# Scores of the next unit but one placed behind the transposes of a unit's first group

## The chip, the cores and the metric

The kernel runs on one core of one Trainium2 chip. The metric is the device time of one execution in microseconds (us), lower is better. Before the change three runs took 3703.43, 3704.79 and 3709.53 us; their median is 3704.79 us.

## What is computed

A macaron layer over 8 sequences of 1024 tokens of width 256: a feed-forward layer with weight 0.5, an attention layer, and the same feed-forward layer again, each behind a layer norm and with a residual.

```python
x = L0_attn_query                                   # (8, 1024, 256)
x = x + 0.5 * ffn(layernorm(x), w_gate, w_up, w_down)
x = x + attn(layernorm(x), Wq, Wk, Wv, Wo, span_val)
x = x + 0.5 * ffn(layernorm(x), w_gate, w_up, w_down)

def attn(query, Wq, Wk, Wv, Wo, span_val):          # 16 heads of 64
    q, k, v = split(query @ Wq), split(query @ Wk), split(query @ Wv)
    w = softmax(q @ k.T / 64 + causal)
    mask = clip((arange(s) + span_val * s) / 33, 0, 1)
    w = w * mask
    w = w / (sum(w) + 1e-8)
    return merge(w @ v) @ Wo

def ffn(x, w_gate, w_up, w_down):                   # inner width 704
    # every operand is quantised to FP4 in blocks of 16 and back before its product
    return fp4_linear(silu(fp4_linear(x, w_gate)) * fp4_linear(x, w_up), w_down)
```

## The kernel before

The program is written out for each engine by hand, with semaphores. It runs in stages: the weights are prepared, the first feed-forward pass runs, then the attention, then the second feed-forward pass. The change touches the attention alone.

The attention (`attention`) goes over the 8 sequences and, in each, over 8 pairs of attention heads, 64 pairs in all (`over_pairs`; loops in the program, with the first and the last of them written out). A pair is cut into 16 units (`UNITS`): one head and one block of 128 rows of queries, in the order of blocks 7, 0, 5, 1, 6, 3, 4, 2 for each of the two heads. Since the attention is causal, unit (a, j) has 128 (j + 1) columns of scores. A unit's work is this:

- scores (`scores`, L1137, L1138, L1141): TensorE multiplies the queries with the upper and the lower half of the keys (32-bit operands split in two), one chunk of up to 512 columns at a time, 8 of the 16 units having two chunks, and adds the causal mask with one 16-bit matmul of 128 columns. There are two PSUM areas, `s_ps[n % 2]`, so the scores of unit n+2 wait until the exponentials of unit n have been taken from the same area (`exp_done`);
- the row maximum on VectorE (`row_max`, L1319) and the exponentials on ScalarE (`exp`, L1233), which go to `e_rows`;
- transposes of the exponentials in groups of up to four blocks of 128 columns (`turn`, L1151; 24 groups a pair), 32-bit, into `t_ps[i % 3]`; the first of a unit waits for the unit's exponentials, and each for the PSUM buffer that group i-3 leaves (`eT_lo`). ScalarE copies the upper half out as 16-bit (`turn_hi`, L1240), VectorE the rest (`turn_lo`, L1325);
- value products three groups later (`value`, L1167): for each block a matmul of 132 columns with the upper half and one of 66 with the lower half; ScalarE copies the result out (`copy_out`, L1251).

Between them stand side pieces that use one PSUM bank, `side_ps`: transposes of the normalised x (L1097), projections of queries and keys for the next pair (L1066), its values (L1078), transposes of the outputs of the pair before (L1105) and their output product (L1115). Each is copied out in two halves by ScalarE (L1213) and VectorE (L1287) or by VectorE alone, and the next piece waits for that.

The order of all this is written by `pair_steps`, which every engine goes through, taking its own kinds of step. For each unit n it puts `scores` of unit n+2 first, then for each of the unit's one or two groups i: `turn` i, `lo` of group i-1, `max` of unit n+2 (first group only), `value` of group i-3, with `copy` where a unit's last group is done, then the side pieces that `slots` gives to group i; `exp` of unit n+2 comes last. The slots are `WO_SLOTS` in even pairs, `V_SLOTS` in odd ones and `FRESH_SLOTS` in the last pair of a sequence. A step's place in the list is its place in the order of its engine; engines meet at semaphores only.

Of the kernel before, what the change touches and what calls it, by code (L numbers as in the profile page):

```python
# [633 lines left out]
def pair_steps(before, after, fresh, values, rows=False):  # L634

    q, k, v, turn_o, wo, turn_x = ([(kind, c, dg) for c in range(n)] for kind, n, dg in (
        ("q", 2, 1), ("k", 2, 1), ("v", 4, 1), ("o_turn", 2, -1), ("wo", 4, -1), ("x_turn", 4, 1)))
    pieces = (turn_x if fresh else []) + (q + k if after else [None] * 4) + (turn_o if before else [None] * 2)
    if values:
        pieces += v if after else [None] * 4
    else:
        pieces += wo if before else [None] * 4
    slots = {i: [] for i in range(NG)}
    for i, piece in zip(FRESH_SLOTS if fresh else V_SLOTS if values else WO_SLOTS, pieces, strict=True):
        slots[i].append(piece)  # L650
    steps, late_hi, late_lo = [], [], []

    def flush(late):
        steps.extend(late)
        late.clear()

    for n in range(NU):
        more = n + 2 < NU or after
        unit = ((n + 2) % NU, (n + 2) // NU)
        if more:  # L660
            steps.append(("scores",) + unit)
        for i in [i for i, (m, _, _) in enumerate(GROUPS) if m == n]:
            first = GROUPS[i][1] == 0
            flush(late_hi)
            steps.append(("turn", i, 0))
            if i or before:
                steps.append(("lo", (i - 1) % NG, (i - 1) // NG))
            flush(late_lo)
            if first and more:
                steps.append(("max",) + unit)  # L670
            if i >= LAG or before:
                steps.append(("value", (i - LAG) % NG, (i - LAG) // NG))
                m = GROUPS[(i - LAG) % NG][0]
                if LAST_GROUP[m] == (i - LAG) % NG:
                    steps.append(("copy", m, (i - LAG) // NG))
            if before and i in NORM:
                steps.append(("norm", NORM.index(i), -1))
            if rows and i >= ROWS_FROM:
                steps.append(("norm_x", i - ROWS_FROM, 1))
            for piece in slots[i]:  # L680

                flush(late_hi)
                flush(late_lo)
                if piece:
                    steps.append(piece)
                    late_hi.append((piece[0] + "_hi",) + piece[1:])
                    late_lo.append((piece[0] + "_lo",) + piece[1:])
        if more:
            steps.append(("exp",) + unit)
    flush(late_hi)  # L690
    flush(late_lo)
    if not after:
        steps.append(("lo", NG - 1, 0))
        for i in range(NG - LAG, NG):
            steps.append(("value", i, 0))
            if LAST_GROUP[GROUPS[i][0]] == i:
                steps.append(("copy", GROUPS[i][0], 0))
    return steps
# [153 lines left out]
def attention(nc, src, dst, dram, keep):  # L852

    with ExitStack() as ctx:
# [201 lines left out]
        def _(pe):  # L1056
# [123 lines left out]
            def pair(b, r, par, before, after, fresh, twin):  # L1180
                g = b * PAIRS + r

                pe.wait_ge(sem("wo_added"), g * 2 - (2 if par else 4) + AHEAD["wo_added"])
                pe.wait_ge(sem("v_masked"), g * 2 + (2 if par else 4))
                prev = ("k_lo", 2 * g + 2)
                for kind, i, dg in pair_steps(before, after, fresh, par == 1, starts_rows(b, r)):
                    if kind == "scores":
                        scores(i, g + dg, par ^ dg)
                    elif kind == "turn":
                        turn(i, g)  # L1190
                    elif kind == "value":
                        value(i, g + dg, par ^ (dg & 1))
                    elif kind == "x_turn":
                        prev = piece(kind, i, b * QT + QT, b * 4 + 4, 1 - par, 1 - par, prev)
                    elif kind in PIECES:
                        prev = piece(kind, i, g + 1, g - 1, 1 - par, 1 - par, prev)
# [13 lines left out]
        def _(act):  # L1210
# [49 lines left out]
            def pair(b, r, par, before, after, fresh, twin):  # L1260
                g = b * PAIRS + r
                for kind, i, dg in pair_steps(before, after, fresh, par == 1, starts_rows(b, r)):
                    if kind == "exp":
                        exp(i, g + dg, par ^ dg)
                    elif kind == "turn":
                        turn_hi(i, g)
                    elif kind == "copy":
                        copy_out(i, g + dg)
                    elif kind == "x_turn_hi":
                        piece("x_turn", i, b * 4 + 4, None)  # L1270
                    elif kind.endswith("_hi"):
                        piece(kind[:-3], i, g + 1, g - 1, 1 - par)
# [10 lines left out]
        def _(dve):  # L1283
# [82 lines left out]
            def pair(b, r, par, before, after, fresh, twin):  # L1366
                g = b * PAIRS + r
                for kind, i, dg in pair_steps(before, after, fresh, par == 1, starts_rows(b, r)):
                    if kind == "norm_x":
                        norm_x(b + 2, i)  # L1370
                    elif kind == "max":
                        row_max(i, g + dg)
                    elif kind == "lo":
                        turn_lo(i, g + dg)
                    elif kind == "norm":
                        normalise(i, g - 1, 1 - par)
                    elif kind == "x_turn_lo":
                        piece("x_turn", i, b * 4 + 4, None)
                    elif kind.endswith("_lo"):
                        if kind == "wo_lo" and i == 0:  # L1380

                            dve.wait_ge(sem("acc_loaded"), b * 16 + (0 if isinstance(r, int) and r == 0 else 16))
                        piece(kind[:-3], i, g + 1, g - 1, 1 - par)
# [67 lines left out]
```

## Time and profile before

| | |
|---|---|
| median of three runs | 3704.79 us |
| the profiled execution | 3706.25 us, its span 3704.5 us |
| mean granted TensorE clock | 0.984 |
| TensorE matmuls | 3460.5 us (93%), 29924 instructions |
| TensorE weight loads | 3147.8 us (85%) |
| VectorE | 2913.8 us (79%) |
| ScalarE | 2278.6 us (62%) |
| GpSimd | 827.0 us (22%) |

The profile names the engines PE (TensorE matmuls), PEld (TensorE weight loads, which run beside matmuls), DVE (VectorE), ACT (ScalarE), POOL (GpSimd) and SP (SyncE, which issues the DMAs). The busy times are sums over the whole span. A matmul's duration reaches from its start to the end that the profile models for it, so that neighbouring matmuls overlap; how much time one takes in the stream is read from its start to the start of the next one. In a timeline a line that ends in x4 stands for four instructions of one kind.

### The profile page before, as it was taken

The numbers are of one execution on the slowest core, as the hardware profiler recorded it, in microseconds if no ns is written. First come the engines' busy times: TensorE is split into PE (matmuls) and PEld (weight loads), VectorE is DVE, ScalarE is ACT, GpSimd is POOL, SyncE is SP. The second block draws the span as 40 slices with busy tenths as digits, with TensorE's granted clock in tenths as the row PEclk, the third lists the DMA queues.
The fourth block names the chain that finished last, engine by engine and source line by source line (L and its number), as shares of the span: only waits on it lengthen the run. The fifth ranks groups of instructions, "written<-read, shape, count | busy, mean of one in ns | idle before, by whom it ended". The sixth has DMA issues, their size and how long they took to land. (4 is left out here: it accounts for less than half of the span.)

```text
span 3704.5 us, 87366 instructions
## 1 busy us (share of the span) xinstructions
PE 3460.5 (93%) x29924; PEld 3147.8 (85%) x29924; DVE 2913.8 (79%) x4756; ACT 2278.6 (62%) x4086; POOL 827.0 (22%) x834
## 2 busy tenths in 40 slices
PE   0799995999999999999999999999999999599998
PEld 0799995888888888888888888888888888499998
DVE  7899983777877787777777778777777777599996
ACT  1445542777777677767767767776777767254554
POOL 2233221121212212122212212212122112123322
PEclk9999998999999999999999999999999999799999
DMA  6211113454544454454545545545534543211111
GB/s 204 76 57 51 51 43 108 104 119 102 145 112 102 119 128 113 107 140 103 119 104 137 119 103 126 119 102 133 125 91 111 134 103 86 97 47 54 51 51 35
DMA packets 157957, 373.40 MB, mean 101 GB/s; under 512 B 19216, under 2 KB 61072, under 8 KB 157200
## 3 DMA queue, kind: packets, MB, share of 16 engines
q1 hardware_dynamic: 157712, 370.30, 39.1%
q8 instruction: 134, 2.20, 0.3%
q14 instruction: 111, 0.91, 0.1%
HBM read 129.31 MB, written 39.58 MB: 46 GB/s over the span
## 5 line engine op out<-in xcount | busy, mean ns | idle before, releaser
L1240 ACT ACTIVATE at_eT_hi<-at_t_ps 128x512 f16<-128x512 f32 (+3 forms) x1536 | 742.4, 490 | 508.9 <-PE at_t_ps L1151 490.8
L1325 DVE SCALAR_TENSOR_TENSOR at_eT_lo<-at_t_ps,at_eT_hi 128x512 f16<-128x512 f32 (+3 forms) x1536 | 824.7, 548 | 127.6 <-ACT at_eT_hi L1240 112.5
L1233 ACT ACTIVATE at_e_rows<-at_s_ps,at_neg_max 128x1024 f32<-128x1024 f32 (+7 forms) x1024 | 761.5, 744 | 95.5 <-DVE at_neg_max L1319 75.2
L1319 DVE TENSOR_REDUCE at_neg_max<-at_s_ps 128x1 f32<-128x1024 f32 (+7 forms) x1024 | 766.9, 749 | 50.1 <-PE at_s_ps L1141 49.8
L1151 PE MATMUL at_t_ps<-at_ident,at_e_rows 128*128 128x128 f32 x4608 | 773.9, 277 | 0.9 <-DVE at_eT_lo L1325 0.9
L1137 PE MATMUL at_s_ps<-at_kh_st,at_q_st 128*128 128x512 f32 (+2 forms) x1536 | 582.3, 379 | 33.9 <-issue 22.9
L1167 PE MATMUL at_o_ps<-at_v_cols,at_eT_hi 128*128 128x132 f16 x4608 | 610.5, 221 | 0.9 <-ACT at_o_raw L1251 0.9
L1167 PE MATMUL at_o_ps<-at_v_cols,at_eT_lo 128*128 128x66 f16 x4608 | 567.9, 193 | 0.0
L1138 PE MATMUL at_s_ps<-at_kl_st,at_q_st 128*128 128x512 f32 (+2 forms) x1536 | 514.1, 342 | 0.0
L1151 PEld LDWEIGHTS at_t_ps<-at_ident,at_e_rows 128*128 128x128 f32 x4608 | 498.9, 141 | 10.5 <-issue 1.4
L1167 PEld LDWEIGHTS at_o_ps<-at_v_cols,at_eT_hi 128*128 128x128 f16 x4608 | 436.0, 98 | 1.8 <-DVE at_eT_lo L1325 0.7
L1167 PEld LDWEIGHTS at_o_ps<-at_v_cols,at_eT_lo 128*128 128x128 f16 x4608 | 420.9, 98 | 17.6
L1066 PE MATMUL at_side_ps<-at_xT_hi,at_w_qk 128*128 128x512 f32 x1012 | 385.3, 421 | 14.5 <-DVE at_q_lo L1287 6.7
L1137 PEld LDWEIGHTS at_s_ps<-at_kh_st,at_q_st 128*128 128x128 f32 x1536 | 290.0, 189 | 69.2 <-issue 26.6
L1030 POOL TENSOR_TENSOR at_o_sum<-at_o_raw 128x1056 f32<-128x1056 f32 x64 | 133.1, 2079 | 835.1 <-ACT at_o_raw L1251 835.1
L1138 PEld LDWEIGHTS at_s_ps<-at_kl_st,at_q_st 128*128 128x128 f32 x1536 | 291.7, 190 | 24.4
L425 POOL TENSOR_TENSOR ffn_h_q<-ffn_code,ffn_scale 128x704 f32<-128x704 f32 x128 | 175.4, 1391 | 585.8 <-DVE ffn_code L366 585.8
L530 PE MATMUL ffn_gu_ps<-ffn_w_gu_hi,ffn_xT_hi 128*128 128x352 f32 x1024 | 262.3, 337 | 14.5 <-DVE ffn_raw L329 10.0
L467 ACT ACTIVATE ffn_silu<-ffn_gu_ps 128x704 f32<-128x704 f32 x128 | 97.1, 759 | 282.1 <-PE ffn_gu_ps L530 282.1
L530 PE MATMUL ffn_gu_ps<-ffn_w_gu_lo,ffn_xT_hi 128*128 128x352 f32 x1024 | 250.3, 326 | 0.0
L530 PE MATMUL ffn_gu_ps<-ffn_w_gu_hi,ffn_xT_lo 128*128 128x352 f32 x1024 | 249.8, 325 | 0.0
L1066 PEld LDWEIGHTS at_side_ps<-at_xT_hi,at_w_qk 128*128 128x128 f32 x1012 | 193.2, 191 | 59.7 <-DVE at_q_lo L1287 21.3
(185 smaller groups left out, 7045.7 us busy)
## 6 DMA issues: line engine op xcount, KB each, us to landing
at_kh_st<-at_k_hi SPq DMA_DIRECT2D x256, 256.0 KB, 4.5
at_kl_st<-at_k_lo SPq DMA_DIRECT2D x256, 256.0 KB, 5.8
at_w_qk<-w_qk_split SPq DMA_DIRECT2D x65, 512.0 KB, 6.2
at_q_st<-at_q_hi SPq DMA_DIRECT2D x128, 256.0 KB, 3.9
at_q_st<-at_q_lo SPq DMA_DIRECT2D x128, 256.0 KB, 4.9
at_w_v<-w_v_split SPq DMA_DIRECT2D x66, 256.0 KB, 5.7
at_w_out<-w_out_split SPq DMA_DIRECT2D x32, 512.0 KB, 3.7
ffn_x_rows<-in_L_attn_query_dram SPq DMA_DIRECT2D x32, 256.0 KB, 2.8
```

The lines of the kernel that those rows point to most:

```text
L425: nc.gpsimd.tensor_tensor(blocks_of(h_q[:, par, j, :INNER]), blocks_of(code[:, j * INNER:(j + 1) * INNER]), per_block(scale[:, par, j * HB ...
L530: last = nc.tensor.matmul(gu_ps[:, c, 0:HALF_I], xT[a][:, par, kt, j * P:(j + 1) * P], gu[b][:, kt, c * HALF_I:(c + 1) * HALF_I], start=n ...
L1030: nc.gpsimd.tensor_tensor(o_sum[:], o_raw[:, :, :VHI], o_raw[:, :, VHI:], ALU.add).then_inc(sem("o_sum"), 1)
L1066: last = nc.tensor.matmul(bank[:], wts[:, w, s, kt, :], xT[t][:, kt, c * CHUNK:(c + 1) * CHUNK], start=i == 0, stop=i == len(passes) - 1)
L1137: nc.tensor.matmul(out, qs, kh_st[par][a][:, k0:k0 + w], start=True, stop=False)
L1138: last = nc.tensor.matmul(out, qs, kl_st[par][a][:, k0:k0 + w], start=False, stop=not lastc)
L1151: last = nc.tensor.transpose(t_ps[i % TBUF][:, b * P:(b + 1) * P], e_rows[:, n % 4, (k0 + b) * P:(k0 + b + 1) * P], ident[:])
L1167: last = nc.tensor.matmul(o[:, :VPART[s]], eT[s][:, i % EBUF, b * P:(b + 1) * P], v_cols[par][:, k0 + b, a, :VPART[s]], start=k0 + b == 0 ...
L1233: nc.scalar.activation(e_rows[:, n % 4, :w], s_ps[n % 2][:, col:col + w], ACT.Exp, bias=neg_max[:, n % 4:n % 4 + 1]).then_inc(sem("exp_don ...
L1240: nc.scalar.activation(eT[0][:, i % EBUF, :count * P], t_ps[i % TBUF][:, :count * P], ACT.Copy, scale=PSCALE).then_inc(sem("eT_hi"), 1)
L1319: nc.vector.tensor_reduce(neg_max[:, n % 4:n % 4 + 1], s_ps[n % 2][:, col:col + P * (j + 1)], AX.X, ALU.max, negate=True).then_inc(sem("ma ...
L1325: nc.vector.scalar_tensor_tensor(out=eT[1][:, i % EBUF, :count * P], in0=t_ps[i % TBUF][:, :count * P], scalar=PSCALE, in1=eT[0][:, i % EB ...
```

## The change

In `pair_steps` the step `scores` of unit n+2 moves from the head of unit n to a place behind the transposes of the unit's first group: behind `turn`, behind `lo` of the group before, behind the late halves of side pieces, and right ahead of `max` of unit n+2. The condition under which it is issued is the same. `scores` is a step of TensorE alone, so the orders of the other engines stay as they are; on TensorE the first `turn` of a unit and the `scores` change places, and `value` follows the `scores` where it followed the `turn`.

```diff
     for n in range(NU):
         more = n + 2 < NU or after
         unit = ((n + 2) % NU, (n + 2) // NU)
-        if more:
-            steps.append(("scores",) + unit)
         for i in [i for i, (m, _, _) in enumerate(GROUPS) if m == n]:
             first = GROUPS[i][1] == 0
             flush(late_hi)
...
                 steps.append(("lo", (i - 1) % NG, (i - 1) // NG))
             flush(late_lo)
             if first and more:
+                steps.append(("scores",) + unit)
                 steps.append(("max",) + unit)
             if i >= LAG or before:
                 steps.append(("value", (i - LAG) % NG, (i - LAG) // NG))
```

## Rows read from the trace of the kernel before

**Rows 1.** Busy time by window: us, then each engine's busy us (instructions), clock, DMA.

```profile
644.00:3154.00 2510.00, 2459.01 (x22978) 2171.32 (x22977) 1941.95 (x3512) 1774.92 (x3473) 503.56 (x536) 1.00 0.48 115
```

**Rows 2.** Groups by line, TensorE, 1000 to 1500 us: count, busy us, mean ns, idle.

```profile
L1137 PE MATMUL at_s_ps<-at_kh_st,at_q_st 128*128 128x512 f32 (+2 forms) x308 | 116.2, 377 | 3.2 <-issue 2.3 <-DVE at_acc L1313 0.6
...
L1138 PE MATMUL at_s_ps<-at_kl_st,at_q_st 128*128 128x512 f32 (+2 forms) x308 | 102.8, 341 | 0.0
```

**Rows 3.** Timeline of TensorE's matmuls, around unit 6: start us, duration us, instruction.

```profile
1012.90 0.19 PE L1167 MATMUL at_o_ps<-at_v_cols,at_eT_lo 128*128 128x66 f16 x1
1012.93 0.22 PE L1167 MATMUL at_o_ps<-at_v_cols,at_eT_hi 128*128 128x132 f16 x1
1013.00 0.19 PE L1167 MATMUL at_o_ps<-at_v_cols,at_eT_lo 128*128 128x66 f16 x1
1013.02 0.48 PE L1137 MATMUL at_s_ps<-at_kh_st,at_q_st 128*128 128x512 f32 x1
1013.35 0.39 PE L1138 MATMUL at_s_ps<-at_kl_st,at_q_st 128*128 128x512 f32 x1
1013.57 0.40 PE L1137 MATMUL at_s_ps<-at_kh_st,at_q_st 128*128 128x512 f32 x1
...
1014.04 0.23 PE L1141 MATMUL at_s_ps<-at_causal,at_ident_b 128*128 128x128 bf16 x1
1014.11 0.61 PE L1151 MATMUL at_t_ps<-at_ident,at_e_rows 128*128 128x128 f32 x4
1014.55 0.22 PE L1167 MATMUL at_o_ps<-at_v_cols,at_eT_hi 128*128 128x132 f16 x1
```

**Rows 4.** Timeline of TensorE's weight loads at the same place.

```profile
1013.00 0.19 PEld L1137 LDWEIGHTS at_s_ps<-at_kh_st,at_q_st 128*128 128x128 f32 x1
1013.11 0.19 PEld L1138 LDWEIGHTS at_s_ps<-at_kl_st,at_q_st 128*128 128x128 f32 x1
```

**Rows 5.** Timeline of TensorE's matmuls, scores behind a projection.

```profile
1510.42 0.39 PE L1066 MATMUL at_side_ps<-at_xT_hi,at_w_qk 128*128 128x512 f32 x1
1510.65 0.40 PE L1137 MATMUL at_s_ps<-at_kh_st,at_q_st 128*128 128x512 f32 x1
1510.89 0.40 PE L1138 MATMUL at_s_ps<-at_kl_st,at_q_st 128*128 128x512 f32 x1
```

**Rows 6.** Timeline of TensorE's matmuls, scores behind the last transpose of x.

```profile
1234.44 0.27 PE L1097 MATMUL at_side_ps<-at_ident,at_xn 128*128 128x128 f32 x1
1234.47 0.48 PE L1137 MATMUL at_s_ps<-at_kh_st,at_q_st 128*128 128x512 f32 x1
1234.78 0.40 PE L1138 MATMUL at_s_ps<-at_kl_st,at_q_st 128*128 128x512 f32 x1
```

**Rows 7.** Timeline of TensorE's matmuls, transposes of a second group behind value products.

```profile
1005.48 0.19 PE L1167 MATMUL at_o_ps<-at_v_cols,at_eT_lo 128*128 128x66 f16 x1
1005.50 0.41 PE L1151 MATMUL at_t_ps<-at_ident,at_e_rows 128*128 128x128 f32 x2
1005.75 0.22 PE L1167 MATMUL at_o_ps<-at_v_cols,at_eT_hi 128*128 128x132 f16 x1
```

**Rows 8.** Waits of TensorE's weight loads, 1000 to 1500 us: us, times, longest us.

```profile
PEld at_side_ps L1066 <- DVE at_q_lo L1287: 3.3, 12, 0.3
```

**Rows 9.** Waits of VectorE, 1000 to 1500 us.

```profile
DVE at_eT_lo L1325 <- ACT at_eT_hi L1240: 21.2, 70, 0.7
...
DVE at_neg_max L1319 <- PE at_s_ps L1141: 6.7, 27, 0.3
```

**Rows 10.** Timelines of VectorE, ScalarE and TensorE: from unit 6 to unit 8.

```profile
1014.48 1.21 DVE L1319 TENSOR_REDUCE at_neg_max<-at_s_ps 128x1 f32<-128x1024 f32 x1
...
1016.22 1.12 ACT L1233 ACTIVATE at_e_rows<-at_s_ps,at_neg_max 128x1024 f32<-128x1024 f32 x1
...
1017.40 0.50 PE L1137 MATMUL at_s_ps<-at_kh_st,at_q_st 128*128 128x512 f32 x1
```

## The prediction

> **What bounds the kernel now.** I read the page's head first, then the busy time by windows, to see which engine fills the stretch that the edit touches. The attention stretch, from the first scores at 644 us to 3154 us, is two thirds of the span of 3704.5 us; in it TensorE is busy 2459 of 2510 us, VectorE 1942 and ScalarE 1775 us, at a granted clock of 1.00 [rows 1]. So VectorE and ScalarE have room (77% and 71%), and TensorE sets the pace. But a matmul that waits for its weights counts as busy here, so 98% does not say that nothing can be gained: the reader has to go from busy time to the distance between the starts of neighbouring matmuls. That is what the timelines of TensorE are for [rows 3 to 7]. Last I read who waits for whom on TensorE's weight loads and on VectorE [rows 8, 9], and one place where a unit's head does wait [rows 10].
>
> **What the change does to the order.** Per unit it exchanges two blocks on TensorE. (The head of a unit is here the place where its work begins; a pair is a pair of attention heads, 16 units, and takes some 40 us.) Before: (work X of the unit before), scores of unit n+2, transposes of group one, value products. After: X, transposes, scores, value products. Nothing is added or removed: 1024 units, each with the same matmuls, the same semaphores and the same waits. ScalarE and VectorE keep their orders. Both blocks wait at the head for the same exponentials (those of unit n: the scores to overwrite their PSUM banks, the transposes to read their rows), so the head wait stays where it is. Three things can move: the price of the boundaries between blocks, the time at which the scores are there (later by the transposes, up to 0.44 us), and the time at which the transposes are there (earlier by the scores, up to about 1 us). SyncE, GpSimd and the DMA queues are not passed by anything.
>
> **Boundaries, priced from start to start.** Everything below is at the clock of 1.00.
>
> Scores behind value products: the last value matmul starts at 1013.00, the first score matmul at 1013.02, the second at 1013.35: 0.35 us for the two. In a stream the short value matmul takes 0.03 (1012.90 to 1012.93) and a score matmul of 512 columns 0.22 (1013.35 to 1013.57) to 0.23. So 0.09 to 0.10 us is open. The weight loads tell why: the first load starts at 1013.00 and the second at 1013.11, so a 32-bit load takes about 0.11, and a matmul of 0.03 cannot hide it [rows 3, 4]. I take 0.09.
>
> Scores behind a projection of 512 columns: 0.23 and 0.24 us from start to start, nothing open [rows 5].
>
> Scores behind transposes, the new boundary: the trace has it at the few places where transposes of x stand ahead of a unit. 1234.44 to 1234.47 to 1234.78 is 0.34 for the two; in a stream it is 0.11 (four transposes in 0.44, 1014.11 to 1014.55) plus 0.23. Nothing is open: a transpose lasts as long as the load behind it [rows 3, 6].
>
> Transposes behind the causal matmul, which disappears: that matmul holds 0.07 (1014.04 to 1014.11), where a stream of about as many columns (the 132 of a value matmul) takes 0.05 to 0.06 [rows 3]: 0.015 open.
>
> Transposes behind value products, new at the head: two take 0.25 us (1005.50 to 1005.75) where two in a stream take 0.22: 0.03 open [rows 7]. Behind a projection I take nothing, as for the scores, since its 0.23 is longer still [rows 5].
>
> Value products behind the causal matmul, new, and not in this trace. From below: the 16-bit load of a value matmul is hidden behind 0.03 us of another value matmul [rows 3], so nothing is open and the causal matmul takes its 0.05. From above: the first value matmul starts 0.11 after the last of four transposes (1014.11 to 1014.55 is four times 0.11) [rows 3], which would put 0.06 on every unit; but 0.11 is the length of the transpose itself, so it is no sign of a slow load. I take 0.005 open, near the low end, and keep 0.06 for a rival. A gain below nothing is excluded, since the columns have to stream.
>
> **The sum.** How many heads stand behind value products is counted in the code: a unit's head does so unless a slot puts a side piece on the last group before it. With the slots of even pairs that is 9 of 16 units, of odd pairs 8, of the last pair of a sequence 6; the very first and the very last pair have fewer side pieces and 13 such heads each: 31 x 9 + 24 x 8 + 7 x 6 + 26 = 539. A second way to the same term: on the two lines of the score matmuls, which have the same shapes and counts, the mean is 377 ns on the one that comes first and 341 ns on the other; 36 ns x 308 is 11.1 us in 500 us, or 54 ns for each of its 205 units (8 of 16 units have two such matmuls, the others one: 308 / 1.5), 55 us over 1024 [rows 2]. 539 x 0.09 is 49 us, and the 63 heads behind the transposes of the outputs, which have the same long first matmul (0.50) [rows 10], bring the rest. The two agree.
>
> Heads behind value products: before 0.09 + 0.015, after 0.03 + 0 + 0.005, so 0.07 us each, times 539: 37.7 us. The 485 others: before 0 + 0.015, after 0 + 0.005, so 0.01 each: 5 us. Together some 42 us less on TensorE.
>
> Not all of it is kept. Where TensorE waits for a side piece's second half, it arrives earlier and waits longer: 12 such waits, of 0.27 us on average, in 500 us [rows 8], about 60 in the stretch, take back 0.07 each, 4 us. Heads that wait for an exponential [rows 10] may give back 1 us more. That leaves 37 us.
>
> The profiled execution took 3706.25 us (its span 3704.5): 3706 - 37 = 3669. The median of the runs before, 3704.79, lies 1.5 us below the profiled execution, so the forecast for the median is 3668 us, 1.0% faster.
>
> **Where a rule of the skill stands against this.** The trace shows second score matmuls that start 0.33 us behind the first where 0.23 would do, with the load of their weights begun only as the matmul before starts [rows 3, 4]. The Trainium skill, page "TensorE: Matmul & The Clock Gate", section "Step-by-step: what each phase is for", says that TensorE's queue pulls weight loads ahead of matmuls in flight, so that the next tile's weights load while this one's matmul runs. Read as a full cover, it would make every order of blocks cost the same, and the time would stay at 3705; the rows show a cover of one matmul's length only.
>
> **Rivals.**
>
> The order costs nothing, since what I read as open load time is bound to the score matmuls and goes with them wherever they stand. Then nothing moves: 3705 us. For it: every score block that isn't behind a projection has a long first matmul, also the one behind the transposes of x (0.48) [rows 6]. Against it: the start of that one is early by what its length is long by, and the distance over both is the stream's. Chance 0.06.
>
> The gain is made on TensorE and half lost at waits. For it: GpSimd apart, all engines are chained within 2 units, VectorE alone waited 70 times in 500 us for ScalarE's halves of the transposed rows [rows 9]. Against it: most of these waits end long ahead of TensorE's need. It would give 18 us: 3687 to 3697. Chance 0.12.
>
> The open load moves to the value products. Behind the causal matmul each unit would pay 0.06 instead of 0.005: 1024 x 0.055 = 56 us more, 3668 + 56 = 3724. Decided by whether a 16-bit load hides behind a matmul of 128 columns. Chance 0.04.
>
> The other side: late scores hold the next but one head. The scores end up to 0.44 us later, VectorE's maximum follows them, then the exponentials on ScalarE, and the head of unit n+2 waits for these. VectorE waited for scores 27 times in 500 us, about twice in each pair [rows 9]. At unit 8 the exponentials end at 1017.34 and the head starts at 1017.40 [rows 10]. If two heads in each of the 64 pairs, this one and another, paid the whole 0.44: 128 x 0.44 = 56 us, and 3668 + 56 = 3724. It decides where the slack from scores to maximum to exponentials is under 0.44. Against it: at that very place the scores start for the last time at 1014.04, the maximum only at 1014.48 since VectorE is still at other work, it ends at 1015.69, and the exponentials start at 1016.22: about 0.2 us of slack before it and 0.53 behind it, which are 0.7 together [rows 3, 10]. Chance 0.08, with the milder forms, 3700 to 3730.
>
> **How the numbers follow.** Forecast 0.70, within 3655 to 3690 (0.05 to 0.09 us a head behind value products, nothing to 5 us taken back). Half lost 0.12; nothing moves 0.06; slower for one of two reasons 0.12. The range, 3653 to 3700, takes in the first two. About 0.2% (7 us) is what a measurement of this kernel can tell from no change. Faster by more than that, under 3697: 0.70 + 0.10 = 0.80. Within it: 0.10. Slower: 0.10.
>
> **What would show it.** In the profile after: at heads behind value products the first transpose follows the last value matmul by 0.03 and the first score matmul the last transpose by 0.03, with the second score matmul 0.34 behind that transpose, not more; the first value matmul 0.05 to 0.07 behind the causal one. The span of the attention stretch is shorter by about 37 us and the feed-forward passes are unchanged. The mean of the first score line does not fall: these matmuls stay long and only start earlier. ScalarE waits less for transposes of first groups. Wrong would be: 0.11 between causal and value matmul, waits of heads for the exponentials that are longer than 0.1 us at most pairs, or a maximum that follows the scores directly in all units.

## The result and the profile after

The changed kernel took 3710.91 us in the median of 20 runs (3703.27 to 3716.12), the kernel before 3704.52 us in 20 runs (3700.63 to 3709.53). The ratio is 1.0015, 95% interval 1.0009 to 1.0022: no gain, at most a loss of 0.2%. Forecast were 3668 us and a range of 3653 to 3700. The profiled execution of the changed kernel took 3703.27 us (span 3701.5), the shortest of its runs; a second one, of the same kernel, had a span of 3707.0. So single spans of the two kernels, 3704.5 before, can't be told apart, and I read the traces by their steady part instead.

GpSimd sums the outputs once in each pair (L1030, after the change L1028), so the distance of these sums is the length of a pair. The timeline of GpSimd around 1100 to 1200 us, the kernel before:

```profile
1118.57 2.08 POOL L1030 TENSOR_TENSOR at_o_sum<-at_o_raw 128x1056 f32<-128x1056 f32 x1 [3.88 <-ACT at_o_raw L1251]
...
1157.16 2.08 POOL L1030 TENSOR_TENSOR at_o_sum<-at_o_raw 128x1056 f32<-128x1056 f32 x1 [24.14 <-ACT at_o_raw L1251]
...
1195.47 2.09 POOL L1030 TENSOR_TENSOR at_o_sum<-at_o_raw 128x1056 f32<-128x1056 f32 x1 [3.86 <-ACT at_o_raw L1251]
```

and the changed one:

```profile
1119.18 2.08 POOL L1028 TENSOR_TENSOR at_o_sum<-at_o_raw 128x1056 f32<-128x1056 f32 x1 [3.94 <-ACT at_o_raw L1249]
...
1157.78 2.08 POOL L1028 TENSOR_TENSOR at_o_sum<-at_o_raw 128x1056 f32<-128x1056 f32 x1 [24.12 <-ACT at_o_raw L1249]
...
1196.11 2.08 POOL L1028 TENSOR_TENSOR at_o_sum<-at_o_raw 128x1056 f32<-128x1056 f32 x1 [3.94 <-ACT at_o_raw L1249]
```

Before, the two pairs take 38.59 and 38.31 us, 76.90 together; after, 38.60 and 38.33, 76.93. This length of two pairs is the measure below. It stays the same to 0.03 us, although TensorE's blocks are cheaper. The timeline of TensorE at unit 6 of the changed kernel, the answer to [rows 3]:

```profile
1013.51 0.19 PE L1165 MATMUL at_o_ps<-at_v_cols,at_eT_lo 128*128 128x66 f16 x1
1013.54 0.63 PE L1149 MATMUL at_t_ps<-at_ident,at_e_rows 128*128 128x128 f32 x4
1013.93 0.48 PE L1135 MATMUL at_s_ps<-at_kh_st,at_q_st 128*128 128x512 f32 x1
1014.25 0.40 PE L1136 MATMUL at_s_ps<-at_kl_st,at_q_st 128*128 128x512 f32 x1
...
1014.94 0.23 PE L1139 MATMUL at_s_ps<-at_causal,at_ident_b 128*128 128x128 bf16 x1
1015.01 0.22 PE L1165 MATMUL at_o_ps<-at_v_cols,at_eT_hi 128*128 128x132 f16 x1
```

From the last value matmul to the next one it is 1.50 us, where the same two blocks took 1.55 before (1013.00 to 1014.55) [rows 3]: 0.05 us saved. The weight load of the first score matmul now starts with the last transpose, a little before the matmul itself:

```profile
1013.90 0.19 PEld L1135 LDWEIGHTS at_s_ps<-at_kh_st,at_q_st 128*128 128x128 f32 x1
```

so 1013.90 to 1014.25 is 0.35 for a transpose (0.11) and a score matmul (0.23), with 0.01 open instead of 0.09.

Where did it go? The waits of TensorE's weight loads over 644 to 3154 us (us in total, times, longest), before (the row left out on top, a wait of the causal matmul's load that the profile puts down to nothing, is 110.8 us and 111.5 after):

```profile
...
PEld at_side_ps L1066 <- DVE at_q_lo L1287: 21.3, 55, 3.4
PEld at_s_ps L1137 <- issue: 16.6, 9, 3.0
PEld at_s_ps L1137 <- ACT at_e_rows L1233: 14.2, 37, 1.5
...
PEld at_side_ps L1105 <- DVE at_oT_lo L1287: 2.3, 9, 0.3
```

and after:

```profile
...
PEld at_side_ps L1103 <- DVE at_oT_lo L1285: 27.3, 63, 0.5
PEld at_t_ps L1149 <- issue: 25.3, 36, 2.6
PEld at_side_ps L1064 <- DVE at_q_lo L1285: 23.6, 56, 3.0
...
PEld at_t_ps L1149 <- DVE at_eT_lo L1323: 9.3, 19, 1.3
PEld at_t_ps L1149 <- ACT at_e_rows L1231: 5.5, 9, 0.8
```

The wait for the lower half of the output transposes grew from 2.3 to 27.3 us, from 9 times to 63, once in each pair but the first. The waits at the heads of units grew from 16.6 + 14.2 = 30.8 to 25.3 + 9.3 + 5.5 = 40.1, the query's from 21.3 to 23.6. Together that is 37 us more of waiting.

The place of the large one is unit 7: its second side piece, output transposes, must wait until VectorE has taken the lower half of the first one, issued in unit 6. VectorE's timeline there, after the change:

```profile
1015.21 1.23 DVE L1317 TENSOR_REDUCE at_neg_max<-at_s_ps 128x1 f32<-128x1024 f32 x1
1016.35 0.68 DVE L1323 SCALAR_TENSOR_TENSOR at_eT_lo<-at_t_ps,at_eT_hi 128x512 f16<-128x512 f32 x1
1016.95 0.68 DVE L1285 SCALAR_TENSOR_TENSOR at_oT_lo<-at_side_ps,at_oT_hi 128x512 fp32r<-128x512 f32 x1
```

and TensorE's:

```profile
1017.19 0.19 PE L1165 MATMUL at_o_ps<-at_v_cols,at_eT_lo 128*128 128x66 f16 x1
1017.69 0.33 PE L1103 MATMUL at_side_ps<-at_ident,at_o_norm 128*128 128x128 f32 x1 [0.30 <-DVE at_oT_lo L1285]
```

The maximum of unit 8's 1024 columns starts 0.27 us after the causal matmul that ends the scores (1014.94), which is when these are there; the half of group 9 and the half of the output transposes stand behind it, and the last one ends at 1017.63. TensorE starts its last value matmul at 1017.19 and the output transposes only at 1017.69. In the kernel before, the same maximum started 0.44 after the causal matmul [rows 3, 10], because VectorE was busy: 0.2 us of cover, as the prediction counted, against the 0.39 of the four transposes (1013.54 to 1013.93) that the scores now stand behind.

### The profile page after: what moved, and what is told of

Its sections match the earlier page's. It is cut to its first block and busy times, and to the rows that moved or that the text cites. A ratio compares the mean times of both kernels' runs of the same rounds, so it can differ in the third digit from the quotient of the medians.

```text
span 3701.5 us, 87366 instructions
## 1 busy us (share of the span) xinstructions
PE 3431.3 (93%) x29924; PEld 3114.3 (84%) x29924; DVE 2924.5 (79%) x4756; ACT 2261.4 (61%) x4086; POOL 827.3 (22%) x834
## 5 line engine op out<-in xcount | busy, mean ns | idle before, releaser
L1135 PE MATMUL at_s_ps<-at_kh_st,at_q_st 128*128 128x512 f32 (+2 forms) x1536 | 615.4, 401 | 9.7 <-issue 9.7
L1149 PEld LDWEIGHTS at_t_ps<-at_ident,at_e_rows 128*128 128x128 f32 x4608 | 521.1, 141 | 77.1 <-issue 25.3
L1028 POOL TENSOR_TENSOR at_o_sum<-at_o_raw 128x1056 f32<-128x1056 f32 x64 | 133.2, 2082 | 834.7 <-ACT at_o_raw L1249 834.7
L530 PE MATMUL ffn_gu_ps<-ffn_w_gu_hi,ffn_xT_hi 128*128 128x352 f32 x1024 | 262.0, 337 | 15.0 <-DVE ffn_raw L329 10.2
L1064 PEld LDWEIGHTS at_side_ps<-at_xT_hi,at_w_qk 128*128 128x128 f32 x1012 | 192.6, 190 | 62.6 <-DVE at_q_lo L1285 23.6
```

The source lines that it names most:

```text
L530: last = nc.tensor.matmul(gu_ps[:, c, 0:HALF_I], xT[a][:, par, kt, j * P:(j + 1) * P], gu[b][:, kt, c * HALF_I:(c + 1) * HALF_I], start=n ...
L1064: last = nc.tensor.matmul(bank[:], wts[:, w, s, kt, :], xT[t][:, kt, c * CHUNK:(c + 1) * CHUNK], start=i == 0, stop=i == len(passes) - 1)
L1135: nc.tensor.matmul(out, qs, kh_st[par][a][:, k0:k0 + w], start=True, stop=False)
L1149: last = nc.tensor.transpose(t_ps[i % TBUF][:, b * P:(b + 1) * P], e_rows[:, n % 4, (k0 + b) * P:(k0 + b + 1) * P], ident[:])
```

## The experiments

Each was timed 4 to 12 times beside the kernel before (the changed kernel first 20 times); a ratio is to that kernel, whose median lay between 3704.5 and 3707.2 us from one series of measurements to the next, so kernels are compared by ratios or within one series. "Two pairs" is the distance over two of the sums above. In all but the first, the shifted-slot and the short-maximum kernels, a set of units keeps its scores at the head:

```diff
+        if more and n in EARLY:
+            steps.append(("scores",) + unit)
         for i in [i for i, (m, _, _) in enumerate(GROUPS) if m == n]:
...
             if first and more:
-                steps.append(("scores",) + unit)
+                if n not in EARLY:
+                    steps.append(("scores",) + unit)
                 steps.append(("max",) + unit)
```

| kernel | median us | ratio (95%) | two pairs us |
|---|---|---|---|
| before | 3704.52 | | 76.90 |
| changed | 3710.91 | 1.0015 (1.0009 to 1.0022) | 76.93 |
| changed, again | 3707.84 | 1.0002 (0.9992 to 1.0012) | 76.92 |
| unit 6 early | 3695.21 | 0.9964 (0.9951 to 0.9977) | 76.62 |
| unit 14 early | 3711.37 | 1.0013 (1.0004 to 1.0022) | 76.92 |
| units 6, 14 early | 3701.40 | 0.9984 (0.9975 to 0.9993) | 76.66 |
| late: unit 6 alone | 3716.06 | 1.0029 (1.0019 to 1.0039) | 77.23 |
| changed, slots moved | 3743.49 | 1.0098 (1.0082 to 1.0113) | 78.24 |
| before, slots moved | 3749.32 | 1.0116 (1.0101 to 1.0132) | 78.45 |
| changed, four slots moved | 3790.19 | 1.0224 (1.0210 to 1.0238) | 79.79 |
| changed, short maximum | 3687.60 | 0.9946 (0.9932 to 0.9959) | 76.53 |
| before, short maximum | 3696.62 | 0.9974 (0.9963 to 0.9984) | 76.88 |
| late: 0, 1, 4, 7, 10, 12 to 15 | 3694.89 | 0.9967 (0.9955 to 0.9979) | 76.63 |
| late: 2, 3, 5, 8, 9, 11 | 3708.24 | 1.0006 (0.9997 to 1.0015) | 76.95 |
| late: 1, 7, 15 | 3706.11 | 1.0001 (0.9992 to 1.0010) | 76.93 |
| late: 0, 4, 10, 12 | 3699.48 | 0.9983 (0.9974 to 0.9993) | 76.68 |
| late: 4, 10, 12 | 3693.27 | 0.9965 (0.9953 to 0.9977) | 76.61 |
| late: 4, 10, 12, 13, 14 | 3692.81 | 0.9967 (0.9956 to 0.9979) | 76.47 |

**The same kernel again, and units 6 and 14 put back.** `EARLY = (6,)`, `(14,)` and `(6, 14)`.

> The changed kernel once more, as the common ground of the other three runs, and to see whether its first profiled execution (3703 us, the shortest of its runs) is like the rest. Both theories expect 1.001 to 1.002 of the kernel before. Theory A (late halves: the maximum, now later on VectorE, pushes the late halves of side pieces behind it, and TensorE waits at the next side piece) expects the same waits of TensorE for VectorE's output halves as in the first profile, 63 times and some 18 to 27 us, whatever the run. Theory B (clock: the gain is there, but the granted clock falls more often) expects a granted clock under that of the kernel before by 0.005 or more, in a profile that is some 7 us longer than the first.

> The changed kernel with the scores of unit 6 alone back at the head (64 of 1024 units). Theory A: the maximum of unit 8's scores (1.2 us) no longer delays the late half of the first output transposes, so TensorE's wait for it falls from some 27 us to under 8 and the kernel is 12 to 16 us faster than the changed one (18 back, 4 given up for 64 boundaries at 0.07). Theory B and theory C (heads wait for exponentials): no less wait, and 4 us slower than the changed kernel.

> The changed kernel with the scores of unit 14 alone back at the head. Theory A, if the wait at the start of a pair (34 us in the changed kernel against 26 before, at unit 0) is of the same kind: 4 to 8 us back, 4 given up, so within 5 us of the changed kernel. Theory C (the exponentials of unit 0, which follow these scores, hold the head of unit 0): the same size, and ScalarE's waits for the maximum get shorter there. It tells how much of the rest hangs on unit 14; theory B expects 4 us slower.

> The changed kernel with the scores of units 6 and 14 at the head, the other 14 late. Theory A: the sum of the two, 14 to 20 us faster than the changed kernel, which is 0.996 to 0.998 of the kernel before. Theory B: 8 us slower than the changed kernel.

The changed kernel came out at 1.0002, with the same wait in its second trace (27.3 us, 63 times); that speaks against theory B, and its granted clock of 0.984 is that of the kernel before. One unit of sixteen back at the head gives 12.6 us against the changed kernel of the same series, in the expected 12 to 16, and the wait falls:

```profile
PEld at_side_ps L1107 <- DVE at_oT_lo L1289: 12.1, 63, 0.4
```

It did not fall under 8: a part of it hangs on something else. Unit 14 back at the head was 3.5 us slower than the changed kernel, within the 5 us that were given, with two pairs as long as before (76.92). Both together were expected 14 to 20 us faster than the changed kernel and were 6, two pairs taking 0.04 us more than with unit 6 alone, which is 1 us over the kernel; the other 5 us are no longer than what the granted clock does to single executions (see the sum below).

**Unit 6 alone late.** All other units in `EARLY`.

> The kernel before with the scores of unit 6 alone late, in 64 of 1024 units. Theory A: 24 us of waits at the side piece of unit 7 appear, less 4 us for 64 cheaper boundaries: 14 to 20 us slower, ratio 1.004 to 1.006. Rival D gives the same sign, but with the wait at the head of unit 8. If the loss needs all units late, this kernel is within 5 us of the one before.

1.0029, 11 us, with two pairs 0.33 us longer, which is 10.6 us over 32 such lengths; expected were 14 to 20. The sign and the place are right (in its trace the wait for the output's half is 23.9 us, 63 times), so a single late unit in sixteen does harm, and all of it at another unit's side piece.

**The second output transposes one group later.**

```diff
-WO_SLOTS = (0, 2, 4, 7, 9, 11, 13, 16, 19, 21)
-V_SLOTS = (0, 2, 4, 7, 9, 11, 13, 16, 20, 22)
+WO_SLOTS = (0, 2, 4, 7, 9, 12, 14, 16, 19, 21)
+V_SLOTS = (0, 2, 4, 7, 9, 12, 14, 16, 20, 22)
```

and, in the last of the three, slots 2 and 4 as 3 and 5.

> The changed kernel with the second output transposes of a pair one group later (slot 11 to 12) and the first value or output product behind them at slot 14 instead of 13. All scores stay late. Theory A (late halves): TensorE no longer meets the unfinished half at unit 7, which cost 24 us a kernel more than before, so 18 to 28 us faster than the changed kernel, 0.993 to 0.996 of the kernel before. Rival D (the scores of unit 6 are late for a reason of their own, such as the exponentials of unit 8, and the side piece is only where TensorE happens to stand): the wait moves to the head of unit 8 or to slot 14 and nothing is gained.

> The control: the kernel before with the same two slots moved. Its wait at that place was 7 us, so theory A expects 4 to 8 us at most, 0.998 to 0.999; a gain like that of the changed kernel would say that the slots were bad by themselves and that the late scores had no part.

> Like the changed kernel with the two slots moved, and the second query projection at slot 3 instead of 2 and the first key projection at 5 instead of 4. TensorE waits there for the query's lower half 56 times in the kernel before too (22 us). Theory A, taken as a rule for side pieces in general (a piece must not come before VectorE is through with the half of the one before): 15 to 25 us more than with the first move, about 0.988 to 0.990 of the kernel before. Against it: the keys arrive later for the copies that the next pair needs, but those are far from their use.

All three missed, by 1% and more, and on the other side. Of late scores they say little: with the slots moved the changed kernel is the faster of the two by 6 us (3743.49 against 3749.32, two pairs 78.24 against 78.45), but the intervals of the two ratios overlap. Of the slots they say more: the kernel before, with its slots moved, waits at another place (TensorE's own waits):

```profile
PE at_s_ps L1137 <- ACT at_e_rows L1233: 26.9, 59, 1.9
```

In its trace unit 8's first score matmul stands 0.61 us behind the last value matmul in the steady pairs. The output transposes in unit 7 fill the time in which ScalarE works on unit 8's exponentials; without them TensorE comes to unit 8's head too early. The chain from scores to exponentials that my fourth rival named is real there, and is covered by just this side piece. The expected gain of the slots left that out. The 27 us are more than half of the 43 that this kernel lost; in the changed kernel TensorE's loads wait for VectorE's halves of the exponentials instead, 45.9 us with two slots moved and 95.1 us with four, against 9.3 without; why was not followed up.

**The maximum over 128 columns.** The computation leaves out the other columns of a unit from its maximum.

```diff
-                nc.vector.tensor_reduce(neg_max[:, n % 4:n % 4 + 1], s_ps[n % 2][:, col:col + P * (j + 1)], AX.X, ALU.max,
+                nc.vector.tensor_reduce(neg_max[:, n % 4:n % 4 + 1], s_ps[n % 2][:, col:col + P], AX.X, ALU.max,
```

> The changed kernel with the row maximum taken over the first 128 columns of a unit's scores only, in all units. It leaves out the rest of the columns from the maximum; every other instruction stands. The longest maximum falls from 1.2 us to under 0.3. Theory A: nothing on VectorE stands in front of the late halves any more, so TensorE's wait at unit 7's output transposes (27 us with the changed kernel) falls to under 3 us, and the cheaper boundaries show in full: it is 25 to 38 us faster than its sister below, whereas with the full maximum the two were within 6 us of each other. Theory D (the loss sits in the exponentials' chain and not in VectorE's order) expects the two short ones as close to each other as the two full ones, within 10 us.

> The kernel before with the same short maximum, the sister of the run above. VectorE was not the bound, but 7 us of waits at unit 7 and some at other side pieces go: 5 to 20 us faster than the kernel before, ratio 0.995 to 0.999.

The late scores turn from a loss of 1 to 6 us into a gain of 9 (3696.62 to 3687.60), two pairs from +0.03 to -0.35 us, which is 12 us over the kernel. So a long maximum is what cost those some 12 us. (It could have done so through the exponentials too, which a short maximum also brings forward; that it did not is read from ScalarE's timeline below.) But 9 is not 25 to 38, and the wait for the output's half stayed at 13.7 us, not under 3. TensorE's timeline at the same place, with the short maximum:

```profile
1048.08 0.19 PE L1165 MATMUL at_o_ps<-at_v_cols,at_eT_lo 128*128 128x66 f16 x1
1048.29 0.33 PE L1103 MATMUL at_side_ps<-at_ident,at_o_norm 128*128 128x128 f32 x1
```

0.21 us from the value matmul to the transposes. The kernel before has 0.16 there, at its own full maximum (the pair after that of [rows 10]):

```profile
1055.07 0.19 PE L1167 MATMUL at_o_ps<-at_v_cols,at_eT_lo 128*128 128x66 f16 x1
1055.23 0.33 PE L1105 MATMUL at_side_ps<-at_ident,at_o_norm 128*128 128x128 f32 x1
```

In a stream it is 0.03. So TensorE waited here before the change too, 0.13 us, so short that the list of waits showed it 9 times only; and what unit 7's cheaper head saves, 0.05, is added to that wait.

**Which heads pay.**

> Late scores only in units 0, 1, 4, 7, 10, 12, 13, 14 and 15, whose heads mostly stand behind value products; units 2, 3, 5, 6, 8, 9 and 11 have theirs at the head, full maximum. If the boundary term is right, it is made there alone: 482 heads at 0.07 us is 34 us less on TensorE, of which about 10 are taken back at waits that exist already, so 20 to 26 us faster than the kernel before, ratio 0.993 to 0.995, at least as good as the kernel with unit 6 alone at the head (0.9964).

> The complement: late scores only in units 2, 3, 5, 8, 9 and 11, whose heads mostly stand behind projections or output transposes. By the boundary term there is nearly nothing to gain here, 0.01 us a head, 4 us, and whatever lateness costs outside unit 6 shows without a gain over it: within 6 us of the kernel before, ratio 0.998 to 1.002. Together with the run above it should add up to the kernel with unit 6 alone at the head.

0.9967 and 1.0006: the gain is made at heads behind value products and nowhere else, as the boundary term has it. But it is 12 us, not 20 to 26 (two pairs 0.27 us shorter, 8 us over the kernel).

**Inside and outside three stretches.** From a side piece to the place where TensorE waits for its late half: unit 1 (second query projection), unit 7, and unit 15 (start of the next pair).

> Late scores only in units 1, 7 and 15, each between a side piece and the place where TensorE waits for its late half. TensorE's boundaries get cheaper by 0.07 us at some 150 heads, 10 us. Theory E (taken back at waits that exist already): nothing of it is seen in the time, within 4 us of the kernel before, ratio 0.999 to 1.001, and the waits at the three places grow by as much as the boundaries save. The rival, that a cheaper boundary is kept wherever it stands and the loss is spread over VectorE, expects 10 us, 0.997.

> Late scores only in units 0, 4, 10 and 12, whose heads stand behind value products in nearly every pair and outside the three stretches. 250 heads at 0.07 us are 17 us. Theory E: kept nearly in full, 12 to 18 us faster than the kernel before, ratio 0.995 to 0.997, as good as the late scores of nine units (0.9967). The rival that spreads the loss evenly expects 6 us at most, 0.998 or more.

Inside them nothing is kept: 1.0001, two pairs 76.93. At unit 7 the wait is 0.21 us again, where the kernel before has 0.16:

```profile
1054.70 0.19 PE L1169 MATMUL at_o_ps<-at_v_cols,at_eT_lo 128*128 128x66 f16 x1
1054.91 0.33 PE L1107 MATMUL at_side_ps<-at_ident,at_o_norm 128*128 128x128 f32 x1
```

Outside, 0.9983 missed the 0.995 to 0.997. The trace names the unit at fault. At the start of a pair the kernel before goes from the last value matmul to unit 0's scores in 0.06 us:

```profile
1035.83 0.19 PE L1167 MATMUL at_o_ps<-at_v_cols,at_eT_lo 128*128 128x66 f16 x1
1035.89 0.49 PE L1137 MATMUL at_s_ps<-at_kh_st,at_q_st 128*128 128x512 f32 x1
```

this one needs 0.16 to unit 0's first transpose:

```profile
1035.45 0.19 PE L1169 MATMUL at_o_ps<-at_v_cols,at_eT_lo 128*128 128x66 f16 x1
1035.61 0.32 PE L1153 MATMUL at_t_ps<-at_ident,at_e_rows 128*128 128x128 f32 x1
```

and the changed kernel the same 0.16. The last pair of runs put that to the test.

> Late scores only in units 4, 10 and 12. If the loss at the start of a pair is unit 0's own: 3 x 0.055 us in 62 pairs is 10 us faster than the kernel before, ratio 0.9965 to 0.998, a little better than with unit 0 (0.9983), and a pair takes 0.16 us less. If the other three bring it: the wait at unit 0 is as long as with four late units and the gain is 4 us, 0.999.

> Units 13 and 14 late as well. Unit 13 stands behind value products in odd pairs, unit 14 in even ones, so one more head of 0.055 us in each pair: 13 to 14 us faster than the kernel before, ratio 0.9955 to 0.997, and a pair takes 0.22 us less. If time saved behind the last side piece of a pair is taken back at the start of the next one, it is no better than the run above.

Three late units, without unit 0, are at 0.9965: better than the same three with it, and as good as any set with the full maximum. In its trace the scores of unit 0 follow the last value matmul by 0.07 again (1034.45 to 1034.52). So the loss at the start of a pair is unit 0's own. Units 13 and 14 added shorten two pairs by another 0.14 us, 4.5 us in all, but the timed ratio (0.9967) does not show it. By their two pairs the kernels should be 9 us (0.29 x 31) and 13 us (0.43 x 31) faster than before; the second is what was timed, the first was timed 4 us better. Its profiled execution is one in which the granted clock fell less often than in the one before (see the sum below); whether that holds for its timed runs is not shown.

## Why the prediction was wrong, point by point

**The order and the boundaries: right in kind.** The new boundaries came out within 0.02 us of what was read from the rows of before: 0.03 to the first transpose, 0.01 open between transposes and scores, 0.07 from causal to value matmul. That last one was taken at 0.055 to 0.06 and is as long as its 0.07 before the change, so nothing was gained there; the head behind value products saves 0.05 (1.55 to 1.50), not 0.07. Over 539 heads that is 27 to 30 us, not 38, and the 5 us of the other heads, which hung on the causal matmul getting cheaper, did not come: the kernel with six such units late is at 1.0006. First mis-sized term: 42 us on TensorE should have been about 30.

**The side pieces: the step that failed.** The prediction followed the late scores along one chain, maximum, exponentials, next head but one, and found 0.7 us of slack in it. That slack is there. The exponentials of unit 8 start 3.17 us behind the last value matmul ahead of unit 6 (1013.51), and 3.22 in the kernel before (1013.00 to 1016.22) [rows 3, 10]:

```profile
1016.68 1.12 ACT L1231 ACTIVATE at_e_rows<-at_s_ps,at_neg_max 128x1024 f32<-128x1024 f32 x1
```

They come no later, so the rival of late heads had no part in the loss there. (The list of waits can't show it, since its sums for exponentials go both ways: 14.2 to 5.5 us on TensorE's loads, 5.6 to 10.2 on its matmuls, the latter at unit 0 of every second pair.) What it did not follow is VectorE's queue behind the maximum: the lower halves stand there, and the output's half at unit 7 had no slack at all, since TensorE was already 0.13 us early for it. Counted from the same value matmul, the maximum starts 0.22 us later (1.48 before, 1.70 after) and the output's half 0.23 later (3.44 after, 1013.51 to 1016.95; 3.21 before):

```profile
1016.21 0.69 DVE L1287 SCALAR_TENSOR_TENSOR at_oT_lo<-at_side_ps,at_oT_hi 128x512 fp32r<-128x512 f32 x1
```

Unit 6's cheaper head brings TensorE there 0.05 earlier, and both together are the 0.28 by which the wait grows, in nearly every pair. From start to start at unit 7: 0.16 before, 0.49 after (1055.54 to 1056.03 in the pair of the rows above), 0.21 where the maximum is short:

```profile
1055.54 0.19 PE L1165 MATMUL at_o_ps<-at_v_cols,at_eT_lo 128*128 128x66 f16 x1
1056.03 0.33 PE L1103 MATMUL at_side_ps<-at_ident,at_o_norm 128*128 128x128 f32 x1 [0.30 <-DVE at_oT_lo L1285]
```

That is 0.28 us a pair, 17 us over 62 pairs. Not all of it lengthens a pair: from the output transposes of unit 7 to the first value product of unit 8 the same pair takes 1.70 us, and 1.79 where only unit 6 is early and the wait is 0.22, because there TensorE waits at unit 8's head instead (the exponentials end at 1055.12 and the transposes start at 1055.25, where the changed kernel has 1056.15 and 1056.52). Of the 0.27 between these two waits 0.09 come back there and 0.05 at unit 6's head, which leaves 0.13, and unit 6 back at the head shortens a pair by 0.15. The prediction stopped at one consumer.

**What is taken back: mis-sized.** The prediction had 5 us for this, by the waits that the list shows with their full length. The runs show three places at which saved time is lost: 0.04 at unit 1 (23.6 - 21.3 us over 56 waits), 0.05 at unit 7, 0.10 at the start of a pair (0.06 to 0.16), 0.19 a pair or some 12 us in all. The list of waits had shown only one of the three as frequent (12 times in 500 us) [rows 8], since a wait that lies within the duration that the profile gives the matmul before it leaves no idle time.

**The sum again.** 27 to 30 us are saved at heads, 17 and 12 lost, and 4 come back ahead of unit 8's values (1.77 us before, 1.70 after). That is 2 to 5 us less, where two pairs are 0.03 us longer (76.90 to 76.93), 1 us over the kernel: as near as a dozen readings to 0.01 us, 62 times over, can come. The timed medians differ by 6 us (1.0015) and by 1 us in the second series (1.0002), more than the 1 us of the pairs. The traces show what can move single executions by so much: the granted clock. The distance of two sums at the end of a sequence, where a pair has more side pieces, is some 45 us where the clock stays at 1.00 and 1.6 to 2 more where it falls to 0.96, and which of them it hits differs between executions of one kernel. Two such pairs of the kernel before and the first of the two in the changed one, busy time by window (clock is the third number from the end):

```profile
1233.80:1278.90 45.10, 42.19 (x378) 36.76 (x379) 32.28 (x58) 28.81 (x58) 7.87 (x8) 1.00 0.44 108
1548.60:1595.70 47.10, 43.84 (x379) 38.12 (x380) 32.28 (x58) 28.88 (x58) 7.88 (x9) 0.96 0.42 103
```

```profile
1234.50:1281.20 46.70, 43.57 (x378) 37.73 (x379) 32.35 (x58) 28.78 (x58) 7.88 (x8) 0.96 0.43 104
```

Between the first and the last of the 64 sums lie 2466.6 us before and 2468.1 in both profiled executions of the changed kernel. These two differ by 5.5 us all the same (3701.5 and 3707.0), and the difference lies behind the last sum (541.9 and 547.7 us), where the granted clock from 3154 to 3215 us was 0.66 in the one and 0.56 in the other. So 6 us between medians are of the size of such falls; whether the late scores change how often they come is not shown.

**The rivals.** That the gain is half lost at waits was the nearest in kind, but all of it went. Open load moving to the value products: no, 0.07 as before. Loads pulled ahead far enough to make every order equal: no. The trace shows the load of the scores beginning with the transpose before, and the kernel with three late units, which moves nothing but this boundary, has two pairs 0.29 us shorter, 0.05 for each of its six late heads. What the Trainium skill says of loads that are pulled ahead ("TensorE: Matmul & The Clock Gate", section "Step-by-step: what each phase is for") holds here for one matmul's length.

**A better version.** With late scores in units 4, 10 and 12 alone the kernel took 3693.27 us, 0.35% less than before (0.9965, 0.9953 to 0.9977). With unit 6 alone at the head it is 0.9964, and with units 4, 10, 12, 13 and 14 late 0.9967 with the shortest two pairs (76.47 us); the times don't tell these three apart. The short maximum is faster still (0.9946) but leaves part of the computation out.

## What to carry to other kernels

When an operation on the pacing engine is moved later, list everything that stands behind its consumer in the consumer's queue, not only what its own result feeds, and for each ask how early the pacing engine comes for it. Time saved between a piece of work and the place where the same engine waits for that piece's copy is not kept; save it outside such stretches. And read such waits from start to start: a wait of 0.1 us behind a matmul of 0.2 us shows no idle time in a list of waits.

## What the hardware showed that was not expected

At the start of a pair, TensorE needs 0.16 us from the last value matmul to a first transpose, but 0.06 to first scores, in the same place and behind the same pair-start waits; elsewhere a head's transpose follows after 0.03. In every second pair both wait for the exponentials of unit 0, and there the scores start 0.05 us behind their end in the kernel before (1074.42 to 1074.47) and the transposes 0.13 behind it with units 0, 4, 10 and 12 late (1073.92 to 1074.05). The transposes have one semaphore wait more in front (for the PSUM buffer), which no run here separates from other causes. It costs more than unit 0's boundary saves.
